# A power of three numbers as GpSimd's rest between indirect requests, in place of 64 index numbers

## What is computed

```
x = x + xattn0(norm(x), ctx)      # top-32 cross attention, a state-space layer, a GELU block
x = x + ffn0(norm(x))             # fast feed-forward with attention: the stages that change
x = x + xattn1(norm(x), ctx)      # 16-head cross attention
x = x + ffn1(norm(x))             # 8 experts, top 4, and a shared one

def fff(x, nw, nb, w1, b1, w2, b2, act):      # x is sent down a tree of depth 8 to one of 256 leaves
    node = 0
    for _ in range(8):
        node = 2 * node + 1 + (x . nw[node] + nb[node] > 0)
    leaf = node - 255
    h = act(x @ w1[leaf] + b1[leaf])          # 16 hidden units
    return h @ w2[leaf] + b2[leaf]

ffn0: q, k, v = fff(xn, q_*), fff(xn, k_*), fff(xn, v_*)      # relu
      y = xn + softmax(q k^T / 16) v
      result = y + fff(y, f_*)                                # gelu
```

## Time and profile before

| | us |
|---|---|
| median of three runs | 1382.71 (1381.66 to 1383.93) |
| span of the profiled execution, first to last instruction | 1503.4 |
| TensorE (matmul) busy | 1203.0, 80% |
| VectorE busy | 887.9, 59% |
| ScalarE busy | 580.3, 39% |
| GpSimd busy | 466.2, 31% |

### The profile page before, as it was taken

One profiled execution on the slowest core, in us unless ns is written; L12 is line 12 of the kernel. 1 busy time (PEld: TensorE's weight loads), 2 busy tenths in 40 slices (PEclk: granted clock), 3 DMA queues, 4 the chain that ended last, 5 costly groups with the idle time before them and its releaser, 6 DMA issues. The chain is left out here.

```text
span 1503.4 us, 24492 instructions
## 1 busy us (share of the span) xinstructions
PE 1203.0 (80%) x7028; PEld 869.8 (58%) x7032; DVE 887.9 (59%) x2553; ACT 580.3 (39%) x1116; POOL 466.2 (31%) x749
## 2 busy tenths in 40 slices
PE   2597999999857756584958793868999989999997
PEld 1395677777646545373746672655666645555554
DVE  8998999999234643452625363565766634453534
ACT  2324566665322113252635331634666641212110
POOL 2237344555450336326141704622221000000000
PEclk9858999999979978697978896876999999999999
DMA  9000000000007412383823731625100000000000
GB/s 267 0 2 1 1 1 1 1 1 1 1 8 192 143 43 80 107 252 97 262 80 91 259 101 56 96 70 136 16 13 10 2 1 1 14 0 14 0 14 15
DMA packets 92463, 91.98 MB, mean 61 GB/s; under 512 B 27057, under 2 KB 77747, under 8 KB 92341
## 3 DMA queue, kind: packets, MB, share of 16 engines
q1 hardware_dynamic: 80052, 65.32, 14.5%
q0 software_dynamic: 12288, 25.18, 6.8%
HBM read 75.79 MB, written 14.68 MB: 60 GB/s over the span
## 5 line engine op out<-in xcount | busy, mean ns | idle before, releaser
L2263 PE MATMUL gq_psH<-gq_xT,gq_w 128*128 (+1 forms) x564 | 102.9, 309 | 53.3 <-ACT gq_act L1981 28.4
L2263 PEld LDWEIGHTS gq_psH<-gq_xT,gq_w 128*128 128x128 f32 x564 | 83.4, 209 | 81.6 <-issue 76.6
L3503 ACT ACTIVATE m_silu<-m_psG 128x512 f32<-128x512 f32 x48 | 28.7, 597 | 215.3 <-PE m_psU L3623 215.3
L2273 PE MATMUL gq_psY<-leaf_w,gq_hT 128*128 (+1 forms) x282 | 95.2, 422 | 20.0 <-issue 14.3
L3556 DVE TENSOR_TENSOR m_act<-m_silu,m_psU 128x512 f32<-128x512 f32 x48 | 33.0, 687 | 122.5 <-ACT m_silu L3503 107.7
L1865 POOL DMA_INDIRECT gq_x<-rows_x,gq_token_i x48 | 47.0, 979 | 174.0 <-PE gq_psX L2252 105.6
L3623 PE MATMUL m_psG<-m_xnT,m_gate 128*128 128x512 f32 x192 | 91.2, 597 | 2.1 <-PEq L192 2.1
L3623 PE MATMUL m_psU<-m_xnT,m_up 128*128 128x512 f32 x192 | 91.4, 599 | 0.0
L2149 DVE SCALAR_TENSOR_TENSOR gq_hT<-gq_xT,unit_leaf,gq_act 128x128 f32<-128x128 f32 x141 | 49.6, 352 | 61.7 <-issue 28.6
L1981 ACT ACTIVATE gq_act<-gq_psH,leaf_b 128x128 f32<-128x128 f32 x141 | 51.4, 365 | 75.4 <-remote 41.5
L783 DVE MATCH_REPLACE8 s_product_a_rest<-a_top,s_product_a_rest 128x256 f32<-128x256 f32 x192 | 76.1, 408 | 0.3 <-issue 0.3
(11 more groups left out here) (574 smaller groups left out, 3063.6 us busy)
## 6 DMA issues: line engine op xcount, KB each, us to landing
leaf_w<-in_group_w SPq DMA_DIRECT2D x128, 128.0 KB
leaf_w<-in_group_w SPq DMA_DIRECT2D x64, 256.0 KB
a_w<-in_L_xattn_W SPq DMA_DIRECT2D x2, 1024.0 KB, 11.9
rows_x<-token_rows SPq DMA_DIRECT2D x8, 256.0 KB, 5.4
sorted_y_q<-gq_y SPq DMA_DIRECT2D x16, 128.0 KB, 3.9
sorted_y_k<-rows_ahead SPq DMA_DIRECT2D x16, 128.0 KB, 4.4
sorted_y_v<-gq_y SPq DMA_DIRECT2D x16, 128.0 KB, 1.7
rows_f<-token_rows SPq DMA_DIRECT2D x8, 256.0 KB
```

Source lines behind the costliest of these rows:

```text
L2263: last = pe.matmul(psH[n % 2][:, 0:P], w1[n % 3][:, c, :], xT[:, c, bass.ds(g * -P + u * P, P)], start=(c == 0), stop=(c == DC - 1))
L2273: pe.matmul(psY[n % 3][:, 0:D], hT[n % 2][:], weights.w2[:, bass.ds(g * D, D)], start=True, stop=True).then_inc(y_ps, 1)
```

## The change

The rest behind an indirect request of `group_products` becomes a power: GpSimd raises a buffer of 128 partitions by 3 numbers, all 1.0, to the power of itself. The first call fills the buffer, and each call waits for the one before. The 16 requests of f's bias rows get such a rest as well, where they had none. Token attention keeps the index numbers, in a class now called `ShortRests`.

```diff
-    def add(self, pool, b):
+    def add(self, pool, b, rest):
         for t in range(b * ST, (b + 1) * ST):
             pool.indirect_dma_start(
                 self.core.x[:, t, :], None, self.core.dram["group_b2"],
                 bass.IndirectOffsetOnAxis(self.leaf_i[:, t, 3:4], 0),
                 compute_op=ALU.add).then_inc(self.added, 16)
-
-    def pool_ahead(self, pool):
+            rest(pool)
+
+    def pool_ahead(self, pool, rest):
         for b in range(B):
-            self.add(pool, b)
+            self.add(pool, b, rest)
...
 class Rests:
+
+
+    def __init__(self, core, ctx, name):
+        self.line = core.sb(ctx, name + "_rest", [P, 3])
+        self.over = core.sem(name + "_rested")
+        self.n = 0
+
+    def __call__(self, pool):
+        if self.n == 0:
+            pool.memset(self.line[:], 1.0).then_inc(self.over, 1)
+        self.n += 1
+        pool.wait_ge(self.over, self.n)
+        pool.tensor_tensor(self.line[:], self.line[:], self.line[:], ALU.pow
+                           ).then_inc(self.over, 1)
+
+
+class ShortRests:
...
-                    beside.pool_ahead(pool)
+                    beside.pool_ahead(pool, rest)
...
-                under_way, rest = [], Rests(core, own, "t")
+                under_way, rest = [], ShortRests(core, own, "t")
```

## The result

| | before | after |
|---|---|---|
| median, us | 1383.32 (1381.66 to 1387.17, 4 runs) | 1441.34 (1436.04 to 1443.59, 4 runs) |
| span of the profiled execution, us | 1503.4 | 1440.4 |

The kernel became slower: the ratio is 1.0414, interval 1.0388 to 1.0440, 57 us (the ratio times the median before; the two medians differ by 58). The forecast was 1351 and the range ended at 1399. The two profiled executions say the opposite, 63 us less. That contradiction is the first thing to clear, and the first experiment does it: the profiled execution of before that the prediction was read from was itself some 120 us slower than the same kernel's other executions.

The account below looks back on a forecast made before the run. It took TensorE as bound, stalled when GpSimd's close requests held back other engines' instruction loads. Of 88.8 us of stalls, 53 were put in plain runs; less 21 us of GpSimd cost, 1382.7 - 32 = 1351, range 1315 to 1399.

Parts of the forecast that it names:

- the way from the profile to the median: Whole kernel: stalls scaled from 88.8 to 53 us for plain runs, GpSimd's 21 us cost left whole, giving 1351.
- the 88.8 us of stalls: 17 TensorE idle times in or just behind GpSimd's unbroken request series, read as held-back instruction loads; 88.8 us.
- The sum in the profiled execution: Whole kernel: 88.8 - 11 - 10 = 68 us less, a profiled execution of 1435 us.
- the signs it named for itself: Stalls gone, TensorE 75% busy in seeds, ScalarE and VectorE without idle over 4 us, token attention 50 to 70 sooner.
- 21 us of cost: GpSimd's longer rests give back 11 us in q, k and v and 10 in f's stage.
- Rival C: GpSimd becomes the limit at v's tiles 11 to 15 and f's end; up to 21 us, 1383 to 1404; 0.17.
- The period: GpSimd's time per request in the sorted products with the power: 2.0 us, bounds 1.85 to 2.15, instead of 1.29.
- The stage without GpSimd's limit: q, k and v with the stalls gone and no GpSimd limit: ends at 742.4, from 820.4 - 78.0.
- the 11 us: q, k and v: part of 78 us of stalls given back, as GpSimd's path ends at 753, not 742.4.
- f's stage: Longer gathers and bias rows there were to win about 1 us and give back 10 of 10.7 us of stall.
- B: Nothing to measure: plain stalls of about GpSimd's 21 us cost, or loads hidden and rests covered; 1383; chance 0.12.
- D: Rests count as traffic, GpSimd's series gets longer, and stalls of 53 us grow by 29: 1412; chance 0.11.

Follow-up runs that it names:

- the first experiment: e1: the kernel before, unchanged, measured and profiled again: 1381.24 us, ratio 1.0011.
- e1: The kernel before with no edit, measured and profiled again: 1381.24 us, ratio 1.0011, profiled span 1379.6 us.
- e2: The kernel before with no rest behind the requests of the sorted products, token attention unchanged: 1380.76 us, ratio 0.9995.
- e5: Against the kernel after: power only behind q's 32 requests, index lists for k and v, f as in the kernel before: 1401.54 us, ratio 1.0159.
- e8: Against the kernel after: four chained index lists instead of the power in q, k and v, f as in the kernel before: 1430.61 us, ratio 1.0369.

## Why the prediction was wrong

**The step that failed is the way from the profile to the median.** The text saw that the profiled execution was 120.7 us longer than the others, and took from it that 53 of the 88.8 us of stalls are in every run. They are in no other execution that was recorded: e1 and e2 show none at the same or a shorter period, and the spans of all the other profiled executions lie within 0.5% of their kernels' medians. Recording by itself adds nothing to see (e1's span of 1379.6 against a median of 1381.24). The gain of 53 us was zero.

**The sum in the profiled execution** came out well, 1435 against a span of 1440.4, but by luck. It took off 88.8 us of stalls, where that execution was 124 us longer than e1, and put on 21 us of cost, where the kernel after is 61 us longer than e1: errors of 35 and 40 us that cancel. Of the signs it named for itself most came true: no stalls, TensorE busy 75% or more in the seeds and the rows ahead, token attention 53 us sooner (820.42 to 767.70), f's bias rows last. One didn't: ScalarE and VectorE have idle times of 12.73 and 13.10 us at the end of v's seeds, as they wait for what TensorE makes of v's 12th tile. It was a comparison of a disturbed execution with an undisturbed one, which no step of the sum could tell. The sign that counted was the one listed as wrong, a profile that is much shorter with a median that isn't.

**Rival C had the mechanism and both places**, v's tiles behind its seeds and the end of f's stage, but at 21 us where 57 were measured. The terms that were mis-sized:

- The period: 2.12 us, not 2.0. The power took 0.89, close to the 0.87 of the middle way; the request itself grew from 0.95 to 1.02, and the gap was 0.18 to 0.20, not 0.16. The stage of q, k and v was to take 753 - 510.1 = 242.9 us and took 252.8. Of this the last of v's gathers came 13.5 us late (720.34 - 514.92 = 205.4 us behind the first, not 192). The 35 units behind it took 34.8 us and not 45, since units without a new tile are the shorter ones (0.99 us each, where v's first eleven turns follow each other by 1.41), and from there to the next stage it was 9.7 and not 2.9, as the rows ahead end last. These two errors partly cancel.
- The stage without GpSimd's limit. It was 820.4 - 78.0, the first profile with its idle times taken off, 232.3 us long. But that execution had lost more than its idle times. TensorE's 47 units between the 12th gathers of k and v took 60.6 us there without the stalls, at a granted clock of 0.85 (661.11 to 739.73), and 53.3 in e1, at 1.00. The stage takes 210.4 us in e1. These 22 us are the larger part of the error: the 11 us become 11 + 10 + 22 = 43, and 42.4 were measured.
- q's pairs were no place in it at all. Alone they make TensorE's last tile of q 18.6 us late (e5), the dearest 32 requests. In the whole change they add nothing to the 43, since GpSimd's path through all requests is the longer one and has them in it.
- f's stage: 1000 - 920.6 = 79 us forecast, 82.8 measured; without the change 70 after the stalls, 68.1 measured in e1. So 10 became 14.7. The f powers, 1.195 us in the mean against 0.914 in "gq", include those behind the bias rows, where the power overlaps the request in the record (932.67 lies inside 931.63 + 1.60); the period there was 2.7 us, as forecast.

**B and D.** B's condition, loads that are hidden, held in all the usual executions recorded, but GpSimd had no slack of the needed size: in q, k and v 51 us for 93. D's direction was right by accident: nothing stretched, since nothing stalled. What made the engines run dry in that one execution **stays open**. The order of events in the earlier trace rows remains what it was, but none of the twelve other profiled executions shows it, and no edit brought it about, so what it takes wasn't found.

## What to carry to other kernels

Before a single wait is priced, compare the profiled execution with the median: where it is 9% longer, record it again, because its idle times, its clock and its pace per unit are all those of another execution. A rest on an engine that only issues requests is priced twice: count times added period, less that engine's own holds, and the delay of the last request that another engine waits for, less the time by which it used to come early. The longer of the two is the cost. So the costs of parts don't add up: two stretches ahead of one barrier share one cover. A pace must be taken where the need is, not over the whole stage: here a tile in 1.57 us at the start of a product, where the mean over its units says 3.3. And where the slack is small, a changed rest is best tried alone in each place, since here 32 of 112 alone cost half.

## What was not expected of the hardware

- Short waits bring the clock down. With waits of 1.6 us for each tile (e5, the longest 2.6) the granted clock went from 0.97 to 0.54 in the same stretch; in the kernel after it was 0.78 over the 68 us of q's pairs. It cost little here: e5's stage is all but 1.6 us as much longer as its last tile is later.
- An indirect request next to a power takes longer, 1.01 to 1.02 us against 0.95 next to index lists (also the median of e8, where single requests take up to 1.51), and its gap is 0.19 against 0.16: 0.1 us a request beyond the power itself.
- A power of 128x1 takes 0.58 us, of 128x3 0.89: three times the numbers for half as much time again.
- Four index lists in a chain have a gap of 0.52 us before the gathers of k and v and 0.54 before v's seeds, but 0.15 before k's seeds and in q's pairs (e8). Why isn't known.
- The kernel before had one execution, a recorded one, of some 120 us more; the ten of e1 lie between 1376.8 and 1390.5 us, and those timed beside the other runs between 1370.2 and 1389.1.
